# Cross attention with a quantized dense layer: the second half's rows loaded whole and split in place, the last sums and the dense layer's loads later in the projection

## What is computed

```python
h = layernorm(x)
q = rope(h @ Wq)                    # [8, 32, 256, 128]
k = rope(ctx @ Wk)                  # 8 heads, each used by 4 query heads
v = ctx @ Wv
p = softmax(where(mask == 0, -1e9, q @ k.T / sqrt(128)))
x = x + (p @ v) @ Wo                # the projection
W = scales * (qweight_4bit - qzeros_4bit)
return x + layernorm(x) @ W + bias  # the dense layer
```

## Time and profile before

| | us |
|---|---|
| median of 3 runs | 2347.29 |
| lowest, highest | 2338.19, 2347.5 |
| the profiled execution | 2343.98 |
| its span, first to last instruction | 2342.2 |
| TensorE busy | 2248.4 |
| VectorE, ScalarE, GpSimd busy | 1351.8, 1042.3, 1379.2 |
| DMA, mean rate over the span | 211 GB/s |

### The profile page before, as it was taken

One profiled execution on the slowest core, in us unless ns is written; L12 is line 12 of the kernel. 1 busy time (PEld: TensorE's weight loads), 2 busy tenths in 40 slices (PEclk: granted clock), 3 DMA queues, 4 the chain that ended last, 5 costly groups with the idle time before them and its releaser, 6 DMA issues.

```text
span 2342.2 us, 33158 instructions
## 1 busy us (share of the span) xinstructions
PE 2248.4 (96%) x10560; PEld 1870.0 (80%) x10560; DVE 1351.8 (58%) x2534; ACT 1042.3 (45%) x2264; POOL 1379.2 (59%) x981
## 2 busy tenths in 40 slices
PE   8998999988999999799999999889999999999999
PEld 6887877767888887688888888668887877878887
DVE  4762574767777776577777777537723234443532
ACT  3222123666766675566677667523322222322000
POOL 1320454567888887688888888655654354354220
PEclk9999999999999999999999999999999999999999
DMA  7676675788788778877878887687554454452111
GB/s 270 234 192 208 229 265 184 235 271 275 241 246 252 242 244 278 281 243 242 255 236 250 250 246 246 189 257 267 189 196 158 148 188 153 152 179 99 46 45 45
DMA packets 310494, 493.52 MB, mean 211 GB/s; under 512 B 28176, under 2 KB 200464, under 8 KB 310416
## 3 DMA queue, kind: packets, MB, share of 16 engines
q1 hardware_dynamic: 289680, 440.12, 58.8%
q10 hardware_dynamic: 19968, 50.34, 6.2%
q0 software_dynamic: 768, 2.10, 0.3%
HBM read 312.09 MB, written 180.37 MB: 210 GB/s over the span
## 4 chain that ended last, share of the span: by engine, by line
PE 65%; DMA 9%; POOL 8%; DVE 8%; issue 3%; ACT 3%; SPq 3%; ACTq 0%; POOLq 0%; DVEq 0%
PE ps L227 14%; PE ps L228 14%; PE ps L229 14%; PE ps L763 8%; PE ps L765 8%; PE ps L764 8%; DMA sq_scratch<-scores 5%; POOL q_t L1540 2%; DMA scores<-in_ctx 2%; POOL rope_tmp L1482 2%; SPq L426 1%; DVE rows L1386 1%; POOL s_buf L1482 1%; POOL q_t L1529 1%; DMA left_scratch<-s_buf 1%
## 5 line engine op out<-in xcount | busy, mean ns | idle before, releaser
L227 PE MATMUL ps<-act_t,wq_t 128*128 128x512 f32 x1280 | 502.4, 393 | 8.5 <-DVE wq_t L1302 4.1
L228 PE MATMUL ps<-act_t,wq_t 128*128 128x512 f32 x1280 | 501.2, 392 | 0.0
L229 PE MATMUL ps<-act_t,wq_t 128*128 128x512 f32 x1280 | 499.2, 390 | 0.0
L763 PE MATMUL ps<-b_parts,a_parts 128*128 128x512 f32 x896 | 353.3, 394 | 17.1 <-POOL b_parts L1558 11.0
L1540 POOL TENSOR_TENSOR q_t<-pt_raw,q_t 128x1024 fp32r<-128x1024 f32 x124 | 298.1, 2404 | 112.1 <-ACT q_t L962 111.1
L1558 POOL TENSOR_TENSOR b_parts<-wraw,b_parts 128x512 fp32r<-128x512 f32 x112 | 195.0, 1741 | 276.2 <-ACT b_parts L984 276.2
L1280 DVE TENSOR_TENSOR a_parts<-xring,a_parts 128x1024 fp32r<-128x1024 f32 x112 | 147.4, 1316 | 355.2 <-ACT a_parts L979 355.2
L764 PE MATMUL ps<-b_parts,a_parts 128*128 128x512 f32 x896 | 350.1, 391 | 0.0
L765 PE MATMUL ps<-b_parts,a_parts 128*128 128x512 f32 x896 | 350.0, 391 | 0.0
L979 ACT ACTIVATE a_parts<-xring 128x1024 fp32r<-128x1024 f32 x112 | 118.7, 1060 | 421.7 <-PE ps L765 413.2
L227 PEld LDWEIGHTS ps<-act_t,wq_t 128*128 128x128 f32 x1280 | 242.2, 189 | 57.7 <-issue 4.7
(11 more groups left out here) (120 smaller groups left out, 4344.4 us busy)
## 6 DMA issues: line engine op xcount, KB each, us to landing
sq_scratch<-scores SPq DMA_DIRECT2D x124, 512.0 KB, 4.9
pt_raw<-sq_scratch SPq DMA_DIRECT2D x496, 128.0 KB, 3.1
xring<-left_scratch SPq DMA_DIRECT2D x112, 512.0 KB, 4.0
left_scratch<-s_buf SPq DMA_DIRECT2D x64, 640.0 KB, 5.1
wraw<-in_L_xattn_Wq SPq DMA_DIRECT2D x64, 512.0 KB, 4.8
wraw<-in_L_xattn_Wo SPq DMA_DIRECT2D x64, 512.0 KB, 4.8
v_scratch<-kv_t ACTq DMA_DIRECT2D x32, 512.0 KB, 2.9
k_scratch<-kv_t ACTq DMA_DIRECT2D x32, 512.0 KB, 4.8
```

What stands on the lines that cost most here:

```text
L227: eng.matmul(dst, lh, rh, start=(k == first), stop=False)
L228: eng.matmul(dst, lh, rl, start=False, stop=False)
L229: mm = eng.matmul(dst, ll, rh, start=False, stop=(k == last))
L763: pe.matmul(dst, lh, rh, start=(begins and not onto), stop=False, skip_group_check=True)
```

## The change

1. `xp_scratch`, the splitting in groups 0 and 1 and its loads and stores are gone; group 1 joins the loop. In group 7, units 2 and 4, ScalarE issues 4 loads each from `xc_scratch` into the low half of `act_t`. ScalarE splits each piece in place into the high half (`split_next`, units 2 to 6), and VectorE takes the rest in place (`rest_of_next`, units 3 to 6). TensorE waits for the low parts.
2. The work on the sums of q = 62 and 63 goes behind the first steps: `combine` after steps 3 and 5 on GpSimd, the stores before `load_step(5)` and `load_step(7)` on SyncE.
3. The dense layer's loads go from s = 5 to s = 20, the dequantization from s = 8 to 32 to s = 23 to 47. The waits in front of those loads fall away.
4. In the last two units VectorE does `step_lo` ahead of `tail_low`.

The diff, cut to its core:

```diff
@@ -157,6 +156,11 @@
+        def next_rows(i, part):
+            c, k = i // 4, i % 4
+            return act_v[:, part, 2 * k:2 * k + 2, c * CT:(c + 1) * CT]
         rope_half = [rope_tmp, s_buf[:, 0:2 * NW].rearrange("p (a n) -> p a n", a=2)]
@@ -438,13 +442,7 @@
-            def load_centred(i):
-                if i > 0:
-                    sp.wait_ge(parts_stored, i * 32)
-                sp.dma_start(x_pair[0], xc_dram[i]).then_inc(xc_in, 16)
-            def attention(G, half, first=False, last=False, switch=False, piece=None):
+            def attention(G, half, first=False, last=False, switch=False):
                 g, nh = (0, 1) if switch else (G - half * 8 + 1, half)
@@ -486,14 +484,9 @@
                             sp.dma_start(rope[:, c, :, :], rope_dram[1, c]).then_inc(rope_in[c], 16)
-                    if piece is not None and u8 % 2 == 1 and piece + u8 // 2 < 7:
-                        load_centred(piece + u8 // 2 + 1)
                 if last:
...
                     load_step(3)
-                    for q in (62, 63):
-                        store_outputs(q, 31, q % 2)
-                        store_sums(q, 31, q % 2)
@@ -538,16 +528,16 @@
             for s in range(4, STEPS):
+                if s in (5, 7):
+                    q = 62 + (s - 5) // 2
+                    store_outputs(q, 31, q % 2)
+                    store_sums(q, 31, q % 2)
                 load_step(s)
...
                     sp.dma_start(rows[:, r, :], x_rows[row_tile(r)]).then_inc(rows_in[r // 8], 16)
-                if s == 5:
-                    for i in range(2):
-                        sp.wait_ge(o_stored[i], 32 * 32)
-                    sp.wait_ge(sums_stored, 64 * 16)
-                    sp.wait_ge(o_copied, UNITS_B)
-                    sp.wait_ge(tail_lo, HB)
+                if s == 20:
                     sp.dma_start(packed, qweight).then_inc(dense_in, 16)
@@ -706,16 +696,14 @@
                     if switch and u8 in (4, 6):
-                        for k in range(2):
-                            pe.wait_ge(xp_in[2 * (u8 - 4) + k], 32)
+                        pe.wait_ge(next_lo, 2 * (u8 - 4) + 2)
                     query(pair, i, 0, G * UPG + (u8 + 4))
...
                     if switch and u8 in (4, 6):
-                        for k in range(2, 4):
-                            pe.wait_ge(xp_in[2 * (u8 - 4) + k], 32)
+                        pe.wait_ge(next_lo, 2 * (u8 - 4) + 4)
                     query(pair, i, 1, G * UPG + (u8 + 4))
@@ -868,14 +856,16 @@
-            def split_piece(i):
-                act.wait_ge(xc_in, (i + 1) * 16)
-                act.activation(x_pair[1].bitcast(F32R), x_pair[0], ACT.Copy).then_inc(piece_hi, 1)
-            def store_parts(i):
-                act.wait_ge(piece_lo, i + 1)
-                act.dma_start(xp_dram[i, 0], x_pair[1]).then_inc(parts_stored, 16)
-                act.dma_start(xp_dram[i, 1], x_pair[0]).then_inc(parts_stored, 16)
+            def load_next(c):
+                act.wait_ge(xc_stored, 8 * 16)
+                act.wait_ge(q_done, 62 + 2 * c)
+                for i in range(4 * c, 4 * c + 4):
+                    act.dma_start(next_rows(i, 1).bitcast(F32), xc_dram[i]).then_inc(next_in[i], 16)
+            def split_next(i):
+                act.wait_ge(next_in[i], 16)
+                act.activation(next_rows(i, 0), next_rows(i, 1).bitcast(F32), ACT.Copy).then_inc(next_hi, 1)
@@ -992,22 +982,15 @@
                         head_hi(0, G * 32 + (u8 // 4 * 16 + 11 * 16), (q_done, G * UPG + (u8 + 4)))
-                    if piece is not None and u8 % 2 == 1:
-                        store_parts(piece + u8 // 2)
+                    if switch and 3 <= u8 <= 6:
+                        split_next(2 * u8 - 5)
                     if not (last and u8 >= 5):
...
-                        c = u8 // 2 - 1
-                        act.wait_ge(q_done, 62 + 2 * c)
-                        act.wait_ge(parts_stored, 8 * 32)
-                        for k in range(4):
-                            for l in range(2):
-                                act.dma_start(act_v[:, l, 2 * k:2 * k + 2, c * CT:(c + 1) * CT].bitcast(F32),
-                                              xp_dram[4 * c + k, l]).then_inc(xp_in[4 * c + k], 16)
+                        load_next(u8 // 2 - 1)
                     if u8 < UPG - 1:
@@ -1030,8 +1013,8 @@
                         scaled(nG, nxt)
-                    if piece is not None and u8 % 2 == 0:
-                        split_piece(piece + u8 // 2)
+                    if switch and 2 <= u8 <= 5:
+                        split_next(2 * u8 - 4)
@@ -1063,8 +1045,8 @@
                 step_hi(s)
-                if s >= 10 and s % 3 == 1 and s < 34:
-                    dense_hi((s - 10) // 3)
+                if s >= 25 and s % 3 == 1 and s < 49:
+                    dense_hi((s - 25) // 3)
                 if s == 92:
@@ -1174,9 +1156,10 @@
-            def rest_of_piece(i):
-                dve.wait_ge(piece_hi, i + 1)
-                dve.tensor_tensor(x_pair[0].bitcast(F32R), x_pair[0], x_pair[1], ALU.subtract).then_inc(piece_lo, 1)
+            def rest_of_next(i):
+                dve.wait_ge(next_hi, i + 1)
+                dve.tensor_tensor(next_rows(i, 1), next_rows(i, 1).bitcast(F32), next_rows(i, 0).bitcast(F32),
+                                  ALU.subtract).then_inc(next_lo, 1)
@@ -1320,12 +1303,18 @@
                         transpose_squares(G, u8)
+                    if switch and u8 in (4, 6):
+                        rest_of_next(2 * u8 - 6)
+                        rest_of_next(2 * u8 - 5)
                     if u8 < UPG - 1:
...
                         masked(nG, nxt, nh, fresh=first and u8 == 0 or last and nxt >= 6)
+                    if switch and u8 in (3, 5):
+                        rest_of_next(2 * u8 - 6)
+                        rest_of_next(2 * u8 - 5)
                     if b == 0 and not tail:
@@ -1344,12 +1333,10 @@
                         set_mask(u8 - 3, 1)
+                    if last and u8 in (6, 7):
+                        step_lo(u8 - 6)
                     if tail:
                         tail_low(u8)
-                    if piece is not None and u8 % 2 == 0:
-                        rest_of_piece(piece + u8 // 2)
-                    if last and u8 in (6, 7):
-                        step_lo(u8 - 6)
@@ -1421,19 +1407,19 @@
                 step_lo(s)
-                if s == 8:
+                if s == 23:
                     dve.wait_ge(dense_in, 48)
...
                                           ALU.bitwise_and).then_inc(z_step, 1)
-                if s == 9:
+                if s == 24:
                     dve.wait_ge(z_step, NIB)
-                if 9 <= s < 33:
+                if 24 <= s < 48:
                     if s % 3 == 0:
-                        dense_full((s - 9) // 3)
+                        dense_full((s - 24) // 3)
                     if s % 3 == 1:
-                        dense_lo((s - 10) // 3)
+                        dense_lo((s - 25) // 3)
                 if 82 <= s < 90:
@@ -1602,14 +1588,15 @@
-            for q in (62, 63):
-                for part in range(2):
-                    combine(q, q % 2, part)
             right_summed(2)
...
                     right_summed(s + 1)
+                if s in (3, 5):
+                    q = 62 + (s - 3) // 2
+                    for part in range(2):
+                        combine(q, q % 2, part)
             pool.wait_ge(bias_in, 16)
```

More of the change, by code:

```diff
@@ L134, in build @@
         xc_dram = dram("xc_scratch", [8, P, 2, CT])
-        xp_dram = dram("xp_scratch", [8, 2, P, 2, CT])
         rope_dram = dram("rope_scratch", [HALVES, 2, P, 2, CT])
@@ L184, in build @@
         moments_in = [sem(f"moments_in{h}") for h in range(HALVES)]
-        xc_in, xp_in = sem("xc_in"), [sem(f"xp_in{i}") for i in range(8)]
+        next_in = [sem(f"next_in{i}") for i in range(8)]
         rows_in = [sem(f"rows_in{i}") for i in range(2)]
@@ L202, in build @@
         x_centred, x_hi, x_lo, rope_scaled = sem("x_centred"), sem("x_hi"), sem("x_lo"), sem("rope_scaled")
-        piece_hi, piece_lo, parts_stored = sem("piece_hi"), sem("piece_lo"), sem("parts_stored")
+        next_hi, next_lo = sem("next_hi"), sem("next_lo")
         q_done, q_rot, q_sum, q_hi, q_lo = sem("q_done"), sem("q_rot"), sem("q_sum"), sem("q_hi"), sem("q_lo")
@@ L526, in load_step @@
                     sp.dma_start(raw[:, 0:NW], wo[p, 0, :, 0:NW]).then_inc(right_in[s % 2], 16)
-            sp.wait_ge(x_lo, TT)
-            load_centred(0)
-            attention(0, 0, first=True, piece=0)
-            attention(1, 0, piece=4)
-            with sp.Fori(2, 7) as G:
+            attention(0, 0, first=True)
+            with sp.Fori(1, 7) as G:
                 attention(G, 0)
@@ L984, in step_hi, with attention @@
                 act.activation(b_parts[:, s % 2, 0, :], wraw[s % 2][:, 0:NW], ACT.Copy).then_inc(right_hi, 1)
```

(14 more changed lines are left out.)

## The result

The changed kernel takes 2314.5 us (median of 4 runs, 2310.1 to 2315.7) against 2347.4 before: a ratio of 0.9863 (95% interval 0.9834 to 0.9893), 33 us faster. The forecast was 2301 in a range of 2286 to 2326, so the time fell in the range and the gain was 13 us smaller than forecast. The profiled execution took 2310.1 us, span 2308.2.

A forecast was written before the change was run, and what follows sets the result against it. TensorE, busy 96% of the span, was taken as the bound, so gains come from its idle and half-speed time: 27 + 14 + 5 = 46 us off 2344.0, giving a median of 2301 us, range 2286 to 2326.

The forecast's parts named there:

- part 1: Start of attention: taking the pieces' splitting out of groups 0 and 1 gains 27 us of 29 lost.
- Rival 1: Start of attention: losses are the empty pipeline's, not the pieces'; only 14 of 29 us go, 2314 us; chance 0.15.
- part 2: Switch to the second half: halved loads, with splits and subtractions added, gain 14 us; 9.4 of 23.4 stay.
- the walk through the code order: Switch: two token blocks followed with earlier durations and landings of 7 to 8 us; lateness 7.0 us.
- late weighing: Switch: weighing of unit 3 comes 1.0 us late, unit 4 0.6, unit 7 0.4.
- half clock and recovery: Switch: 1.7 us for half clock after the longest wait, 0.7 of recovery, on top of the 7.0.
- Rival 2: Switch: GpSimd is the bound, slowed by VectorE's new subtractions; 4.0 us more, 3.4 with half clock; 2308 us; chance 0.12.
- part 3: End of attention and projection: moved sums, dense loads and the step_lo order together gain 5 us, bounds -4 and 12.
- (a): Projection step 2: with combine(63) moved behind, the 6.2 us wait and 3.4 us of half clock go.
- (d): Last two attention units: step_lo before tail_low makes tail_low(6) 0.9 us later.
- (b): Projection steps 5 to 7: loads behind the sums' stores come 2.4 and 3.2 us late; 8.7 us lost with half clock.
- (c): Dense layer's loads: 4.7 us wait and 1.7 half clock go at step 6; 1.4 us lost at step 20.

The follow-up runs named there:

- the seventh kernel: The changed kernel with VectorE's 8 new subtractions at the switch on half of each piece's columns; 2311.3 us, ratio 0.9854.
- the tenth kernel: The changed kernel with the switch's 8 loads but no splits or subtractions there, TensorE waiting for the landings; 2313.2 us, ratio 0.9864.
- neither: The changed kernel without the switch's 8 loads and without its splits and subtractions; 2305.3 us, ratio 0.9825.
- the first experiment: The changed kernel with last sums, dense loads and order of VectorE's last two units as before the change; 2307.9 us, ratio 0.9844.

## Why the prediction was right, and where it was not

**Right: part 1.** 28.5 us for 27. The reading of the earlier trace rows held: without the wait on the split, group 0 took 58 us. Both causes named, traffic (with its issues) and waiting, are real and about equally large. Rival 1 (a start of the empty pipeline that stays) is out: group 1 runs at 66 us. That its 2314 us is what was measured is chance.

**Too large: part 2.** 9.7 us for 14; 14.9 stay where I had 9.4. The step that failed is the walk through the code order with the durations of the earlier trace rows and one landing of 7 to 8 us. By its terms: TensorE was idle for 9.8 us (147.10 less 137.27) where the walk had 7.0. The turned probabilities took 3.3 of them, for my 2.0 of late weighing, and the subtractions 5.9 in the two second halves of the query, for my 2.9 and 2.1. The other 5.1 us are in the matmuls' own time, for my 2.4 of half clock and recovery: I had counted one stretch at 1.2 GHz, and 10.2 us in two were granted, with the waits of 3.33 and 4.25 us. The half clock is thus half of what the sum missed. The issues were cheaper than I had it (0.65 us) and the landings as assumed:

```profile
L864 ACTq DMA_DIRECT2D act_t<-xc_scratch x8: 527/652/1111, 883.9 to 912.1; - x8
L868 ACT ACTIVATE act_t<-act_t x8: 1039/1042/1047, 895.0 to 928.6; 128x1024 fp32r<-128x1024 f32 x8
L1161 DVE TENSOR_TENSOR act_t<-act_t x8: 1232/1740/2312, 898.5 to 931.2; 128x1024 fp32r<-128x1024 f32 x8
...
DMA to landing us min/median/max: 6.0/7.9/11.1
```

The subtraction took 1.74 us for the 1.23 of the pieces. None of the pieces' 8 had an operation of GpSimd beside it, not even in group 1, where GpSimd was busy for 57 of 82 us; each of the new 8 had one or more. Rival 2 had GpSimd as the loser of that contention; here VectorE's operation is the one that gets longer, and GpSimd's too when VectorE's starts first (L1538 took 1.72 us for 0.74). The Trainium skill (SBUF — State Buffer, "Who interferes with whom") says "Issue order, not op shape, decides who blocks"; that fits both. But the seventh kernel, with half of each subtraction, shows that this price is a small part at most. What the walk had left out is the other half of the loop: the stores and turned loads behind the burst. The chain of work that ended last has a store of scores, issued 2 us after ScalarE's first four loads began to be issued, that landed 10.94 us later, where 4.7 is the median of all:

```profile
886.01 10.94 DMA sq_scratch<-scores
...
898.62 2.91 DVE act_t L1161 x2
```

TensorE's first wait, 3.3 us to 896, is again for the turned probabilities, and the tenth kernel, with its loads alone, shows them late with no work added. The 5 us that stay with neither were in no term.

The prediction said that the trace disagrees with the Trainium skill (DMA: Bandwidth & Descriptors, "Issuing engines are not separate DMA queues"), which calls the time to initiate a DMA usually small beside the DMA. For one transfer the trace agrees: 0.85 us at the median against 11.8 to landing before, 0.65 against 7.9 after. It was eight issues in a row that held ScalarE for 5.8 and 9.4 us, and moving the new ones to SyncE gained nothing.

**Wrong sign: part 3.** -6.7 us for +5. By its steps:
- (a), the 9.6 us of steps 1 and 2: 8.7 gained. Right, though the fourth edit would have brought some 3 of them without the sums' move, which the prediction had only as a cost (d).
- (b), load_step(5) and (7) behind the sums' stores, 8.7 us: 13.6 lost. The mechanism and its two places were right, the size wasn't: GpSimd waited 6.31 and 6.18 us for the loads, and the sum that follows took 2.14 and 1.85 us, not 1.3, with VectorE's subtraction beside it. The waits were 4.7 and 4.2 us for my 2.4 and 3.2, both long enough for half clock behind them, where I had counted one.

GpSimd's timeline after:

```profile
1502.65 2.14 POOL L1556 TENSOR_TENSOR wraw<-wraw 128x512 f32<-128x512 f32 x1 [6.31 <-DMA wraw<-in_L_xattn_Wo]
...
1519.90 1.85 POOL L1556 TENSOR_TENSOR wraw<-wraw 128x512 f32<-128x512 f32 x1 [6.18 <-DMA wraw<-in_L_xattn_Wo]
...
1601.07 2.19 POOL L1556 TENSOR_TENSOR wraw<-wraw 128x512 f32<-128x512 f32 x1 [6.48 <-DMA wraw<-in_L_xattn_Wo]
```

- (c), the dense layer's loads: 6.4 us came back as said; at steps 20 and 21 they cost 5.3 for my 1.4, near the bound of 6.4. The load behind the burst came 6.48 us late for GpSimd (1601.07), where 1.80 is usual: 4.7 us later, not 3.3, and the longer sum and the half clock came on top. The move bought 1.1 us, and 1.0 at the first block's end that I had counted as 0 (3.8 against the first experiment).
- (d), 0.9 us for `tail_low`: the wait grew from 2.8 to 3.8 us. Right. The rest of the 3.1 us that this stretch grew by is scatter, as far as these runs tell.

8.7 - 13.6 + 6.4 - 5.3 + 1.0 - 3.1 - 0.9 (step 0, half clock) = -6.8, which is the table's -6.7.

That the total still fell in the range is due to part 1, which carried most of it, and in part to luck: part 3 came out beyond its own lower bound (-4) by 3 us, and only the width that the other two parts gave the range took that in.

## What to carry to other kernels

Before moving a stall away, walk the queue it goes to: a store that waits for a slow engine, put in front of a load, costs the load its whole head start. The burst of 1.6 MB in front of one step's load, with some 2 us of cover, cost 6.4 us at step 5 and 5.3 at step 20; one transfer to a step cost nothing. When a loop through several engines has two causes of lateness, each can be enough alone: taking one away or halving it shows little, so test with each alone and with neither before a loss is shared out. Take a price from a row where the neighbour's operations overlap the one that is priced: a neighbour that is busy for most of the window can still miss it every time.

## What the runs showed of the hardware

A subtraction of 128 x 1024 on VectorE with both inputs in SBUF took 1.22 to 1.23 us in the 8 cases before in which no operation of GpSimd overlapped it, and 1.23 to 2.31 us, 1.74 at the median, in the 8 after, which all overlapped one. At 909.44 VectorE started 0.1 us ahead of GpSimd and took 1.23 us; GpSimd's sum beside it took 1.70 for 0.74.

Some of TensorE's idle gaps had a stretch at 1.2 GHz, of 3.4 or 6.8 us, that began in the gap or at most 1.5 us behind it. The length of the gap told which only at the ends. From group 0 on, the 14 kernels have 121 gaps of 1.6 us and more: all 49 of 3.44 us and more had such a stretch, none of the 17 of up to 1.81 us, and 29 of the 55 between. Gaps of 2.38 and 2.39 us had none in four kernels and gaps of 2.40 and 2.41 us had one in three others; one of 3.38 us had none.

The stretch before the attention, which no edit reached, varied by 7.4 us from one kernel to the next: as much as several of these edits are worth, so that their sizes had to be read from stretches of the trace and not from the totals.
